# Attention and mixture-of-experts block on one core: the experts' fp32 products made of float32r parts, weights in three sets, and new places for all steps

## The chip, the core and the metric

The kernel runs on one core of one Trainium2 chip. The metric is the device time of one execution in microseconds. Five engines work from queues of their own, each in order: PE (TensorE) multiplies, DVE (VectorE), ACT (ScalarE) and POOL (GpSimd) do element-wise work, SP (SyncE) issues DMAs; POOL issues the indirect ones. Semaphores order them against each other.

## The reference, cut to what matters

```python
x = x + xattn(layernorm(x), ctx, ctx, w_q, w_kv, w_concat)      # x: 16 x 128 x 256, fp32
x = x + ffn(layernorm(x), ...)
# ffn: attn_out = layer_norm(x) * nw + nb
#      top-1 gate over 8 experts, capacity 2048 / 8 = 256 rows each
#      dispatched = the 256 rows (zeros where there are fewer) of each expert
h = gelu(einsum('ecm,emi->eci', dispatched, inter_w) + inter_b[:, None, :])    # 256 -> 1024
expert_out = einsum('eci,eim->ecm', h, output_w) + output_b[:, None, :]        # 1024 -> 256
moe_out = einsum('sec,ecm->sm', combine, expert_out)
rh = gelu(attn_out @ res_inter_w + res_inter_b)                 # the residual MLP, all rows
out = (rh @ res_output_w + res_output_b) * coef[:, :1] + moe_out * coef[:, 1:] + x
```

All operands are fp32.

## The kernel before

The 2048 rows are worked in 8 blocks of 256 (`U = 8`, two tiles `t` of 128 rows each). A block n < 8 goes through attention, gate and residual MLP. Its rows are then scattered into `dispatched` in DRAM by expert (POOL's indirect DMAs, step `gw`). When all blocks have been scattered, the 8 experts follow as n = 8 to 15, each with 256 rows. `weights(n)` gives the residual MLP's weights for n < 8 and a set of the expert's otherwise.

For one expert e (n = 8 + e):

- `ein`: SP loads the expert's rows (`drow`) and its bias (`outb`); PE transposes the rows (4 instructions, L607), ACT scales them into `ao` (L871, two instructions), DVE takes the row numbers (L1076).
- `up(n, c)`, c = 0 to 3: PE makes two 128-column pieces of the inner layer, each the sum of two fp32 products of 128x128 weights (stationary) with 128x256 values (`product`, L612); ACT applies the gelu to each (L890) and writes `h`.
- `down(n, t, q)`, t = 0, 1 and q = 0 to 3: PE adds two products of 128x128 pieces of `h` (stationary) with 128x256 of `w2` (L776). After q = 3, DVE adds the bias (L1093) and multiplies by the row's gate (L1097), and POOL adds the rows to the output by an indirect DMA (L580).
- `wload(e)`: SP loads w1 and w2 of the expert, 1 MB each; one semaphore stands for both. There are four sets (`SETS = 4`).

Which step comes after which is no result of the run: a table of times (`AT0`, `AT1`, `AT` for the blocks, `EXPERT` for the experts, `LOADS`, and a lag per engine) gives every step a planned time, and each engine issues its steps sorted by it. Only the order counts on the chip, not the planned times.

```python
    def order(lag):
        return [step for _, _, step in sorted((place + lag.get(step[0], [0.0])[0], n, step) for place, n, step in steps)]
```

In the middle of the expert stage PE's order is: up(n+1,0), down(n,0,0), down(n,0,1), up(n+1,1), down(n,0,2), down(n,0,3), up(n+1,2), down(n,1,0), ein, down(n,1,1), up(n+1,3), down(n,1,2), down(n,1,3).

The PSUM banks are rings of two per kind: `up` has one ring (`ubank`), freed by the gelu; `down` and the transposes share another (`mbank`).

## Time and profile before

| what | value |
|---|---|
| median of 3 runs | 447.14 us (445.47 to 448.82) |
| profiled execution, its own time | 447.72 us |
| its span | 446.0 us |
| PE busy | 381.6 us, 86% |
| ACT, POOL, DVE busy | 167.6, 153.2, 142.2 us |

The span runs from the first to the last instruction; 1.7 us of the execution's time lie outside it. An engine's busy time is the union of its instructions. PE's instructions overlap one another, so the mean duration of one is longer than the distance from one to the next.

### The profile page before, as it was taken

How to read it: one execution, taken by the hardware profiler on the slowest of the kernel's cores; microseconds unless marked ns; L12 is line 12 of the kernel's file. 1: busy time of each engine (PE TensorE's matmuls, PEld its weight loads, DVE VectorE, ACT ScalarE, POOL GpSimd, SP SyncE). 2: the span in 40 equal slices, each digit the busy share in tenths (PEclk: the TensorE clock that was granted, in tenths of full speed). 3: DMA queues.
4: the chain of work that ended last, by engine and by line, in shares of the span. 5: the costliest groups of instructions: out<-in, count | busy, mean ns of one | idle time of the engine just before them, and what ended most of it. 6: DMA issues, size and time to landing. Idle time of an engine off the chain costs nothing.

```text
span 446.0 us, 5656 instructions
## 1 busy us (share of the span) xinstructions
PE 381.6 (86%) x1978; PEld 292.7 (66%) x1978; DVE 142.2 (32%) x461; ACT 167.6 (38%) x325; POOL 153.2 (34%) x219
## 2 busy tenths in 40 slices
PE   4767777778998788988988988889999899999992
PEld 2435245555676476576576566678888788888881
DVE  3263424532354354363364263241101010101020
ACT  3213334345255435534536525552243223332310
POOL 4322313218156238247238035265002121212122
PEclk9757666986999999998999999999999999999998
DMA  7678650230022462381411410085122775581212
GB/s 203 189 193 233 228 134 2 76 79 24 23 72 77 125 234 71 94 272 51 114 35 61 104 37 12 21 294 165 47 68 64 196 235 166 128 251 12 25 18 29
DMA packets 51331, 49.78 MB, mean 112 GB/s; under 512 B 4764, under 2 KB 48488, under 8 KB 51304
## 3 DMA queue, kind: packets, MB, share of 16 engines
q1 hardware_dynamic: 48232, 45.21, 33.2%
q0 software_dynamic: 3072, 4.21, 5.2%
q8 instruction: 16, 0.26, 0.3%
q14 instruction: 11, 0.09, 0.1%
HBM read 33.65 MB, written 15.63 MB: 111 GB/s over the span
## 4 chain that ended last, share of the span: by engine, by line
PE 65%; DMA 10%; ACT 8%; DVE 7%; issue 5%; POOL 2%; SPq 2%; DVEq 0%; POOLq 0%; ACTq 0%
PE mbank L776 20%; PE ubank L612 18%; PE mbank L612 11%; DMA drow<-dispatched 8%; PE mbank L607 4%; PE pbank L697 4%; ACT p L847 3%; PE sbank L665 3%; PE sbank L687 3%; DVE smax L977 3%; PE pbank L706 2%; DVE core L1021 2%; ACT h L890 1%; DMA wq_raw<-in_L_xattn_w_q 1%; ACT oT L791 1%
## 5 line engine op out<-in xcount | busy, mean ns | idle before, releaser
L890 ACT ACTIVATE h<-ubank,vecT 128x256 f32<-128x256 f32 x128 | 53.7, 471 | 131.7 <-PE ubank L612 131.7
L776 PE MATMUL mbank<-w2r,h 128*128 128x256 f32 x256 | 64.1, 390 | 0.5 <-ACT h L890 0.5
L612 PE MATMUL ubank<-ao,w1r 128*128 128x256 f32 x256 | 62.7, 393 | 0.0
L776 PE MATMUL mbank<-w2e,h 128*128 128x256 f32 x256 | 60.8, 379 | 0.0
L580 POOL DMA_INDIRECT out_rows<-yrow,rowid x16 | 24.8, 1548 | 103.7 <-DVE yrow L1097 73.5
L612 PE MATMUL ubank<-ao,w1e 128*128 128x256 f32 x256 | 60.0, 379 | 0.0
L776 PEld LDWEIGHTS mbank<-w2r,h 128*128 128x128 f32 x256 | 48.4, 194 | 12.8 <-issue 5.3
L612 PEld LDWEIGHTS ubank<-ao,w1r 128*128 128x128 f32 x256 | 49.4, 197 | 6.6
L612 PEld LDWEIGHTS ubank<-ao,w1e 128*128 128x128 f32 x256 | 48.5, 190 | 6.6
L776 PEld LDWEIGHTS mbank<-w2e,h 128*128 128x128 f32 x256 | 48.2, 190 | 6.3
L977 DVE TENSOR_REDUCE smax<-sbank 128x4 f32<-128x512 f32 x64 | 41.9, 685 | 26.5 <-PE sbank L665 26.2
L847 ACT ACTIVATE p<-sbank 128x512 f32<-128x512 f32 x64 | 36.9, 595 | 33.8 <-PE sbank L687 33.7
L1093 DVE TENSOR_TENSOR ytmp<-mbank,outb 128x256 f32<-128x256 f32 x16 | 6.8, 425 | 90.8 <-PE mbank L776 90.8
L665 PE MATMUL sbank<-kstack,qstack 96*128 96x128 bf16 x256 | 25.0, 240 | 8.0 <-DVE smax L977 6.7
L665 PEld LDWEIGHTS sbank<-kstack,qstack 96*128 96x128 bf16 x256 | 18.9, 107 | 16.4 <-DVE smax L977 8.9
L687 PE MATMUL sbank<-qstack,kstack 98*128 98x512 bf16 x64 | 25.0, 418 | 2.2 <-DVE smax L977 1.8
L697 PE MATMUL pbank<-p,vone 128*32 128x512 f32 x128 | 19.1, 671 | 8.2 <-ACT p L847 7.8
L612 PE MATMUL mbank<-xT,wq 128*128 128x256 f32 x64 | 20.2, 470 | 4.2 <-ACT ao L871 3.0
L871 ACT ACTIVATE ao<-mbank,vecT 128x256 f32<-128x256 f32 x32 | 16.3, 561 | 15.3 <-PE mbank L607 15.3
L529 POOL TENSOR_TENSOR yy<-va,mhalf 128x4 f32<-128x4 f32 x8 | 8.4, 1046 | 39.7 <-DVE va L1012 39.7
L612 PE MATMUL mbank<-wc,oT 128*128 128x256 f32 x64 | 18.0, 429 | 4.2 <-ACT oT L791 4.2
L496 POOL TENSOR_TENSOR rs<-va,mhalf 128x2 f32<-128x2 f32 x8 | 5.8, 720 | 45.7 <-DVE va L936 45.7
(123 smaller groups left out, 438.1 us busy)
## 6 DMA issues: line engine op xcount, KB each, us to landing
w1e<-in_L_ffn_inter_w SPq DMA_DIRECT2D x8, 1024.0 KB, 4.9
w2e<-in_L_ffn_output_w SPq DMA_DIRECT2D x8, 1024.0 KB, 8.4
qstack<-dram_q SPq DMA_DIRECT2D x16, 384.0 KB, 4.6
dram_q<-qpart SPq DMA_DIRECT2D x8, 384.0 KB, 2.5
dispatched<-zrow SPq DMA_DIRECT2D x4, 516.0 KB, 5.4
drow<-dispatched SPq DMA_DIRECT2D x8, 258.0 KB, 8.3
xs<-in_x SPq DMA_DIRECT2D x8, 256.0 KB, 4.6
ctxs<-in_ctx SPq DMA_DIRECT2D x8, 256.0 KB, 4.7
```

The costliest lines, as they stand in the source:

```text
L580: pool.indirect_dma_start(out=out[:, :], in_=yrow[:, e % 2, t, :], in_offset=None, compute_op=ALU.add, out_offset=bass.IndirectOffsetOnAxi ...
L607: last = nc.tensor.transpose(dst[:, o:o + P], src[:, t, kc * P:(kc + 1) * P], ident[:, :])
L612: last = nc.tensor.matmul(dst, w[kc], v[kc], start=(kc == 0), stop=(kc == len(w) - 1))
L665: last = nc.tensor.matmul(b[:, i * P:(i + 1) * P], qstack[0:KS, r, t, 4 * (g % HG) + i, :], kstack[0:KS, r, bs], start=True, stop=True)
L687: nc.tensor.matmul(b[:, :], kstack[:, r, bs], qstack[:, r, t, hs:hs + 4, :], start=True, stop=True)\
L697: last = nc.tensor.matmul(b[32 * g:32 * g + 32, :, :], vone[:, u % 3, t, :], p32[:, n % 2, g, :, :], start=True, stop=True, tile_position= ...
L706: last = nc.tensor.transpose(b[:, i, :], o_raw[:, n % 2, i, :], ident[:, :])
L776: last = nc.tensor.matmul(b[:, 0:D], h[:, n % 2, f, t * P:(t + 1) * P], w2[:, f, :], start=(f == 0), stop=(f == FC - 1))
L847: nc.scalar.activation(p32[:, (k // HB) % 2, g % HB, :, :], scores, ACT.Exp, scale=SCALE)\
L871: ins = nc.scalar.activation(ao[:, n % NAO, kc, :], place["cT", n][:, kc * UT:(kc + 1) * UT], ACT.Identity, bias=vecT[:, R_NB + kc:R_NB + ...
L890: nc.scalar.activation(h[:, n % 2, f, :], place["up", n, c][:, j, :], ACT.Gelu_apprx_tanh, bias=vecT[:, col:col + 1]).then_inc(sem("gelu_d ...
L977: V.reduce_max(smax[:, g // HG, hs:hs + 4], place["A", u, g][:, :].rearrange("p (h t) -> p h t", h=4), AX)\
```

## The change

1. A product of an expert is no longer one fp32 product. Both operands are split into a high part (the value written as float32r) and a low part (the value less the high part), and three float32r products are added: high x high, high x low, low x high. The residual MLP and the attention stay as they were.
2. The splits: `ws1` (w1, in four quarters of 128x512: ACT copies the high part, POOL subtracts), `ws2` (w2, likewise: DVE copies, DVE subtracts), `ao` (ACT copies, DVE subtracts), and `h` after each `up` (ACT copies 128x512, DVE subtracts). The low part lies where the value lay; the high parts have tiles of their own, two of each.
3. Three sets of weights in place of four. w1 and w2 are loaded by steps of their own (`w1load`, `w2load`), each as soon as the last user of its own tile is through. `drow` and `outb` have four places in place of eight, so that `ein` of expert 4 and later waits for an earlier expert's end.
4. All planned times and lags are new, those of the attention too, and `o_rec` has two buffers.

```diff
-    SETS = 4
+    SETS = 3
+    EIN = 4
+    Q = 4
...
-        "period": 17.22, "up": [-2.35, 2.53, 4.67, 9.02],
-        "down": [17.16, 18.79, 20.45, 21.34, 23.58, 25.85, 26.32, 28.49], "ein": [9.47], "first": [-3.51],
+        "period": 13.91, "up": [-4.57, -1.85, -1.43, 2.78],
+        "down": [5.15, 7.92, 11.04, 14.37, 16.08, 16.88, 17.07, 17.83], "ein": [11.7], "first": [-2.28],
+        "ws1": [-23.13, -21.33, -21.16, -18.19], "ws2": [-6.23, -5.05, -3.84, 1.18], "w1load": [14.71],
+        "w2load": [36.23],
...
+            def w1load(e):
+                if e >= SETS:
+                    sp.wait_ge(sem("up_done"), C2 * (U + e - SETS + 1))
+                w1, src = (w1r, res_inter_w) if e < 0 else (w1e[e % SETS], inter_w[e])
+                sp.dma_start(w1[:, :, :], src.rearrange("(k p) f -> p k f", p=P))\
+                  .then_inc(sem("w1r_in" if e < 0 else f"w1e_in{e % SETS}"), 16)
+
+            def w2load(e):
+                if e >= SETS:
+                    sp.wait_ge(sem("down_done"), T * (U + e - SETS + 1))
+                w2, src = (w2r, res_output_w) if e < 0 else (w2e[e % SETS], output_w[e])
+                sp.dma_start(w2[:, :, :], src.rearrange("(c p) d -> p c d", p=P))\
+                  .then_inc(sem("w2r_in" if e < 0 else f"w2e_in{e % SETS}"), 16)
+
             def wload(e):
                 if e == 2:
                     sp.wait_ge(sem("x1_ready"), U)
-                if e >= SETS:
-                    sp.wait_ge(sem("down_done"), T * (U + e - SETS + 1))
-                w1, w2 = weights(U + e if e >= 0 else 0)
-                src1 = res_inter_w if e < 0 else inter_w[e]
-                src2 = res_output_w if e < 0 else output_w[e]
-                came = sem("wr_in" if e < 0 else f"we_in{e % SETS}")
-                sp.dma_start(w1[:, :, :], src1.rearrange("(k p) f -> p k f", p=P)).then_inc(came, 16)
-                sp.dma_start(w2[:, :, :], src2.rearrange("(c p) d -> p c d", p=P)).then_inc(came, 16)
+                w1load(e)
+                w2load(e)
...
+                if e >= EIN:
+                    sp.wait_ge(sem("y_ready"), T * (e - EIN + 1))
...
+            def split(e, q):
+                pool.wait_ge(sem("w1_high"), Q * e + q + 1)
+                w = quarter(w1e[e % SETS], q)
+                pool.tensor_tensor(quarter(w1l[e % SETS], q), w, quarter(w1h[e % 2], q).bitcast(f32), ALU.subtract).then_inc(sem("w1_low"), 1)
...
             def up(n, c):
                 w1 = weights(n)[0]
-                if c == 0:
-                    pe.wait_ge(sem("ao_ready"), n + 1)
-                    if n == 0:
-                        pe.wait_ge(sem("wr_in"), 32)
-                    if n >= U:
-                        e = n - U
-                        pe.wait_ge(sem(f"we_in{e % SETS}"), 32 * (e // SETS + 1))
-                b = claim("up", n, c)
-                for j in range(2):
-                    f = 2 * c + j
-                    last = product(b[:, j, :], chunks(w1, slice(f * P, (f + 1) * P)), chunks(ao[:, n % NAO, :, :]))
+                if n < U:
+                    if c == 0:
+                        pe.wait_ge(sem("ao_ready"), n + 1)
+                    if n == 0 and c == 0:
+                        pe.wait_ge(sem("w1r_in"), 16)
+                    b = claim("up", n, c)
+                    for j in range(2):
+                        f = 2 * c + j
+                        last = product(b[:, j, :], chunks(w1, slice(f * P, (f + 1) * P)), chunks(ao[:, n % NAO, :, :]))
+                else:
+                    e = n - U
+                    if c == 0:
+                        pe.wait_ge(sem("ao_low"), e + 1)
+                        pe.wait_ge(sem("w1_low"), Q * (e + 1))
+                    b = claim("up", n, c)
+                    for j in range(2):
+                        f = slice((2 * c + j) * P, (2 * c + j + 1) * P)
+                        wh, wl = chunks(w1h[e % 2], f), chunks(w1l[e % SETS], f)
+                        ah, al = chunks(aoh[:, e % 2, :, :]), chunks(aol[:, n % NAO, :, :])
+                        last = product(b[:, j, :], wh + wh + wl, ah + al + ah)
                 last.then_inc(sem("up_done"), 1)
 
             def down(n, t, q):
                 w2 = weights(n)[1]
+                e = n - U
                 if q == 0:
                     claim("down", n, t)
-                    pe.wait_ge(sem("gelu_done"), FC * (n + 1))
+                    if n < U:
+                        pe.wait_ge(sem("gelu_done"), FC * (n + 1))
+                        if n == 0:
+                            pe.wait_ge(sem("w2r_in"), 16)
+                    else:
+                        pe.wait_ge(sem("w2_low"), Q * (e + 1))
+                if n >= U and t == 0:
+                    pe.wait_ge(sem("h_low"), C2 * e + q + 1)
                 b = place["down", n, t]
                 for f in (2 * q, 2 * q + 1):
-                    last = nc.tensor.matmul(b[:, 0:D], h[:, n % 2, f, t * P:(t + 1) * P], w2[:, f, :],
-                                            start=(f == 0), stop=(f == FC - 1))
+                    if n < U:
+                        last = nc.tensor.matmul(b[:, 0:D], h[:, n % 2, f, t * P:(t + 1) * P], w2[:, f, :],
+                                                start=(f == 0), stop=(f == FC - 1))
+                    else:
+                        hi, lo = hh[:, e % 2, f, t * P:(t + 1) * P], hl[:, n % 2, f, t * P:(t + 1) * P]
+                        wh, wl = w2h[e % 2][:, f, :], w2l[e % SETS][:, f, :]
+                        nc.tensor.matmul(b[:, 0:D], hi, wh, start=(f == 0), stop=False)
+                        nc.tensor.matmul(b[:, 0:D], hi, wl, start=False, stop=False)
+                        last = nc.tensor.matmul(b[:, 0:D], lo, wh, start=False, stop=(f == FC - 1))
...
+                if n >= U:
+                    act.wait_ge(sem("ao_ready"), n + 1)
+                    if n >= U + 2:
+                        act.wait_ge(sem("up_done"), C2 * (n - 1))
+                    copy(aoh[:, n % 2, :, :], ao[:, n % NAO, :, :]).then_inc(sem("ao_high"), 1)
+
+            def split(e, q):
+                if q == 0:
+                    if e == 0:
+                        act.wait_ge(sem("x1_ready"), U)
+                    act.wait_ge(sem(f"w1e_in{e % SETS}"), 16 * (e // SETS + 1))
+                    if e >= 2:
+                        act.wait_ge(sem("up_done"), C2 * (U + e - 1))
+                copy(quarter(w1h[e % 2], q), quarter(w1e[e % SETS], q)).then_inc(sem("w1_high"), 1)
...
+                if n >= U:
+                    if n >= U + 2 and c == 0:
+                        act.wait_ge(sem("down_done"), T * (n - 1))
+                    act.wait_ge(sem("gelu_done"), 2 * (i + 1))
+                    copy(hh[:, n % 2, 2 * c:2 * c + 2, :], h[:, n % 2, 2 * c:2 * c + 2, :]).then_inc(sem("h_high"), 1)
...
+                dve.wait_ge(sem("ao_high"), e + 1)
+                a = ao[:, (U + e) % NAO, :, :]
+                V.tensor_tensor(aol[:, (U + e) % NAO, :, :], a, aoh[:, e % 2, :, :].bitcast(f32), ALU.subtract).then_inc(sem("ao_low"), 1)
+
+            def split(e, q):
+                if q == 0:
+                    if e == 0:
+                        dve.wait_ge(sem("x1_ready"), U)
+                    dve.wait_ge(sem(f"w2e_in{e % SETS}"), 16 * (e // SETS + 1))
+                    if e >= 2:
+                        dve.wait_ge(sem("down_done"), T * (U + e - 1))
+                w = quarter(w2e[e % SETS], q)
+                V.tensor_copy(quarter(w2h[e % 2], q), w).then_inc(sem("w2_high"), 1)
+                dve.wait_ge(sem("w2_high"), Q * e + q + 1)
+                V.tensor_tensor(quarter(w2l[e % SETS], q), w, quarter(w2h[e % 2], q).bitcast(f32), ALU.subtract).then_inc(sem("w2_low"), 1)
+
+            def up(n, c):
+                if n < U:
+                    return
+                i = C2 * (n - U) + c
+                dve.wait_ge(sem("h_high"), i + 1)
+                a = h[:, n % 2, 2 * c:2 * c + 2, :]
+                V.tensor_tensor(hl[:, n % 2, 2 * c:2 * c + 2, :], a, hh[:, n % 2, 2 * c:2 * c + 2, :].bitcast(f32), ALU.subtract)\
+                    .then_inc(sem("h_low"), 1)
```

Sorted by the new tables, one expert of the middle reads, engine by engine (n = 11 is expert 3):

```
PE    up(11,0) down(10,0,2) up(11,1) up(11,2) ein(4) down(10,0,3) up(11,3) down(10,1,0..3) down(11,0,0..1) up(12,0)
ACT   up(11,0) ws1(4,3) up(11,1) up(11,2) ein(4) up(11,3) ws1(5,0..2) up(12,0)
DVE   up(11,0) ws2(3,3) down(10,0) up(11,1) up(11,2) ein(4) down(10,1) up(11,3) ws2(4,0..2) up(12,0)
POOL  ws1(4,0..2) down(10,0) ws1(4,3) down(10,1) ws1(5,0..2)
SP    w1load(5) w2load(4) ein(5) w1load(6) w2load(5) ein(6)
```

Ahead of the experts PE's order is now up(7), ein(0), down(7,0), down(7,1,0), up(8,0), down(7,1,1) and so on; before it was up(7), ein(0), all of down(7), up(8,0). On ACT ws1(0) stands between the steps of up(7), ahead of ein(0); on DVE ws2(0) begins behind down(7,0). In the attention, SP now issues the residual MLP's weights (`wload` of -1) directly ahead of gather(2,0), the load of block 2's queries, where it stood ahead of the first maxima of block 1 before, and PE runs the transpose M of a middle block behind q of a later one, where it stood ahead of it.

## Rows read from the trace of the kernel before

**Rows 1.** The page: span, and busy time of each engine.

```profile
span 446.0 us, 5656 instructions
PE 381.6 (86%) x1978; PEld 292.7 (66%) x1978; DVE 142.2 (32%) x461; ACT 167.6 (38%) x325; POOL 153.2 (34%) x219
```

**Rows 2.** Busy time by stretch: its length, PE, PEld, DVE, ACT, POOL; clock; DMA.

```profile
0.00:286.00 286.00, 235.00 (x1281) 165.79 (x1282) 120.07 (x385) 121.59 (x223) 112.03 (x176) 0.89 0.36 107
...
320.80:437.40 116.60, 114.50 (x541) 99.47 (x539) 13.27 (x38) 33.91 (x78) 23.23 (x15) 1.00 0.43 113
```

**Rows 3.** The chain that ended last, in order of time: start, us, what.

```profile
310.45 2.58 DMA drow<-dispatched
313.81 7.14 PE mbank L776 x32
```

**Rows 4.** The same chain from 400 us on.

```profile
402.40 1.73 PE ubank L612 x8
404.13 1.73 PE mbank L776 x8
...
411.90 0.44 PE mbank L607 x4
...
428.74 8.65 PE mbank L776 x40
```

**Rows 5.** Timeline of PE in the attention: start, length of the group, count.

```profile
255.57 0.61 PE L665 MATMUL sbank<-kstack,qstack 96*128 96x128 bf16 x8
256.02 0.61 PE L706 MATMUL pbank<-ident,o_raw 128*128 128x128 f32 x4
```

**Rows 6.** Single durations by tile (ns, min/median/max), answers for kstack, w1e and ident.

```profile
L665 PEld LDWEIGHTS sbank<-kstack,qstack x256: 95/98/152, 24.6 to 266.7; 96*128 96x128 bf16 x128
...
L612 PEld LDWEIGHTS ubank<-ao,w1e x256: 186/190/192, 320.6 to 428.1; 128*128 128x128 f32 x128
...
L607 PEld LDWEIGHTS mbank<-ident,drow x32: 138/141/144, 313.1 to 412.0; 128*128 128x128 f32 x32
```

**Rows 7.** Timeline of ACT in the expert stage.

```profile
336.97 0.84 ACT L890 ACTIVATE h<-ubank,vecT 128x256 f32<-128x256 f32 x2 [2.61 <-PE ubank L612]
338.27 1.02 ACT L871 ACTIVATE ao<-mbank,vecT 128x256 f32<-128x256 f32 x2 [0.46 <-PE mbank L607]
```

**Rows 8.** Groups by line, engine and shape: count, busy us, mean ns, idle before.

```profile
L580 POOL DMA_INDIRECT out_rows<-yrow,rowid x16 | 24.8, 1548 | 103.7 <-DVE yrow L1097 73.5 <-DVE rowid L1076 30.1
...
L1093 DVE TENSOR_TENSOR ytmp<-mbank,outb 128x256 f32<-128x256 f32 x16 | 6.8, 425 | 90.8 <-PE mbank L776 90.8
...
L1097 DVE TENSOR_SCALAR yrow<-ytmp,drow 128x256 f32<-128x256 f32 x16 | 5.7, 353 | 0.6
...
L954 DVE TENSOR_TENSOR qres<-mbank,qpart 128x512 f32<-128x512 f32 x8 | 5.5, 692 | 27.8 <-ACT qpart L791 27.8
...
L791 ACT ACTIVATE qpart<-qres 128x512 bf16<-128x512 f32 x8 | 5.0, 628 | 3.0 <-DVE qres L954 3.0
```

**Rows 9.** Timeline: DVE's gate steps beside POOL, at two places.

```profile
243.59 1.15 POOL L523 TENSOR_TENSOR qpart<-qres,qpart 128x512 bf16<-128x512 f32 x1
...
243.82 0.96 DVE L1039 SCALAR_TENSOR_TENSOR gkey<-gd,desc 128x16 f32<-128x16 f32 x1
...
298.11 2.56 POOL L538 TENSOR_SCALAR xs<-xs,oneplus,mrs 128x256 f32<-128x256 f32 x2
...
298.91 0.18 DVE L1039 SCALAR_TENSOR_TENSOR gkey<-gd,desc 128x16 f32<-128x16 f32 x1
```

**Rows 10.** Single durations by tile (min/median/max), answer for xs: DVE's tensor_scalar.

```profile
L1021 DVE TENSOR_SCALAR core<-xs,mv,yy x16: 384/540/884, 70.4 to 294.5; 128x256 f32<-128x256 f32 x16
```

**Rows 11.** DMA issues by line: count, KB each, median us from issue to landing.

```profile
w1e<-in_L_ffn_inter_w SPq DMA_DIRECT2D x4, 1024.0 KB, 4.9
w2e<-in_L_ffn_output_w SPq DMA_DIRECT2D x4, 1024.0 KB, 8.4
```

**Rows 12.** Busy time by stretch, as in rows 2, near the kernel's start.

```profile
20.00:40.00 20.00, 14.45 (x70) 9.69 (x70) 9.39 (x20) 4.29 (x9) 4.61 (x7) 0.50 0.67 181
```

More of the change, by code:

```diff
@@ L115, in xattn_moe_ffn_kernel @@
-        "ein": [0.0], "down": [0.25], "zero": [0.0], "late": [-0.64],
+        "load": [3.74], "kspill": [-7.59], "qspill": [-1.22], "gather": [11.52], "M": [0.79], "wload": [-0.23],
+        "ein": [-7.33], "down": [4.67], "zero": [2.93], "late": [-3.31], "w1load": [0.0], "end": [0.19],
+        "small": [0.72], "w2load": [-3.58],
     }
     LOADS = {
-        "late": [-70.79], "vec": [-39.4], "zero": [-46.04, -45.13, -6.03, -0.66],
-        "weights": [0.5, 14.17, 15.87, 27.03, 27.11],
+        "late": [-84.53], "vec": [17.26], "zero": [-38.12, -21.43, -12.78, -4.6],
@@ L588, in _ @@
             calls = {"small": small, "ln1": ln1, "xn": norm_x, "kv": k_parts, "qlast": q_last, "ln2": ln2, "core": residual,
[L589 removed]
+                     "gw": scatter, "bias": bias, "ws1": split, "down": down, "end": end}
             for step in order(LAG_POOL):
```

128 lines of the change are left out of this document (74 added, 54 removed), and 21 rows, old and new, of tables (AT, AT0, AT1).

## The prediction

> **What bounds the kernel now.** I read the page first: PE is busy for 86% of the span, no other engine for 40% [rows 1]. The stretches show where: in the expert stage (320.8 to 437.4 us, 116.6 us) PE is busy for 98% at full clock (granted 1.00, the 2.4 GHz level), ACT for 34 us, POOL 23, DVE 13 [rows 2]. The chain in order of time says the same: from 400 us on it is PE alone, groups of 8 matmuls 1.73 us apart [rows 4]. So one instruction of an expert's product costs 1.73 / 8 = 0.216 us. An expert has 64 of them (each of its 32 products is recorded as two) and four transposes in 0.44 us [rows 4]: 64 x 0.216 + 0.44 = 14.3 us, against 116.6 / 8 = 14.6 measured. The stage costs what PE's passes cost. Ahead of it stands a latency chain through the last block's scatter and the load of the first expert's rows, which land at 313.0 us [rows 3]; the change does not touch it; the attention (286 us, PE busy for 235 [rows 2]) is touched only in its order.
>
> **PE's new price.** A product becomes three float32r matmuls. No trace here shows one. The nearest rows: a bf16 matmul of 128 columns, each with new weights, takes 0.45 / 8 = 0.056 us [rows 5], one pass at 0.44 ns a column; an fp32 instruction of 256 columns takes 0.216, or 0.84 ns a column, two passes. So float32r is between one pass, 0.108 us, and two, 0.216. I take one pass: a format that still needed two would be no format of its own, and three of them would be half again as dear as the fp32 product. Its weight load may show. The load of 128 fp32 columns takes 190 ns as a record and lies wholly behind 0.216 us of streaming; the transposes' single load takes 141 ns at a distance of 0.44 / 4 = 0.11 us; a bf16 load takes 98 at a distance of 0.056 [rows 4 to 6]. In all three the distance is that of the streaming alone, so I take the load as hidden. If it were not, the 128 columns of the load would add their 0.056 to each. Per expert: 96 x 0.108 + 0.44 = 10.8 us, 3.5 less than now.
>
> **ACT's new load**, in order with all it did: gelu 4 x 0.84, affine 1.02 [rows 7], and nine copies of 128x512 (four of w1, four of h, one of ao) at the 0.628 us of the copy of qres [rows 8]: 3.4 + 1.0 + 5.7 = 10.1 us, perhaps 0.2 more for the waits on its own results. That is just under PE. Its copies of h stand between the gelu and the next gelu, which frees PE's bank: a step `up` takes ACT 0.84 + 0.65 = 1.5 us and PE 12 x 0.108 = 1.3, but the down steps lie between, so it holds.
>
> **DVE's new load.** Nine subtractions of 128x512 at 0.69 us (L954) [rows 8]; four copies of 128x512, between 0.48 (the 0.353 of a 128x256 tensor_scalar [rows 8] plus half of the 0.26 that a tensor_tensor takes for 256 more columns, 0.692 - 0.425) and 0.69, as a subtraction; I take 0.55. Two bias additions and two multiplications, 2 x (0.425 + 0.353) [rows 8], and the row numbers, 0.2. Sum 6.2 + 2.2 + 1.6 + 0.2 = 10.2, with a wait of 0.03 ahead of some ten of them 10.5 us (10.2 to 11.1). What stands behind a waiting instruction matters here: DVE waits for PE's down(10,0) and only then does the subtractions of up(11,1) and up(11,2) and of ein(4).
>
> **POOL's new load.** Four subtractions at 1.15 (L523) [rows 9] and two indirect DMAs at 1.55 [rows 8]: 7.7 us. POOL's last quarter of w1 stands behind the scatter of down(10,0), so up(12,0) needs, after PE's last matmul of down(10,0): 0.8 on DVE, 1.55 and 1.15 on POOL, 3.5 us and up to two of DVE's instructions in between. PE has up(11,3), down(10,1) and two steps of down(11,0) for that, 48 matmuls, 5.2 us. It fits while nothing else delays it.
>
> **The two together.** This is what decides. DVE's gate step L1039 handles 16 numbers a row and takes 0.18 us in one place and 0.96 in another. In the slow place POOL runs a tensor_tensor from 243.59 to 244.74, and L1039 ends at 244.78; in the fast one POOL runs a tensor_scalar [rows 9]. Both L1039 and POOL's tensor_tensor read two operands from SBUF. DVE's tensor_scalar shows it too: 384 ns at least, 884 at most [rows 10], where the slow ones stand beside POOL's arithmetic. So DVE's two-operand work does not run beside POOL's two-operand work. The change puts 9 x 0.69 = 6.2 us of the first on DVE and 4 x 1.15 = 4.6 of the second on POOL for each expert, and the four copies and two multiplications (2.9 us) may be held up like the tensor_scalar. If all of it excludes, DVE and POOL together need 10.5 + 4.6 = 15.1 us, less what DVE can do meanwhile (the additions from PSUM, 0.85, and the row numbers), 14.1. If only the two-operand work excludes, the copies and multiplications also fit beside POOL: 11.2, but then they must fall in the right place. I take 13.3 us per expert, nearer the upper end because the long copies resemble the tensor_scalar that was held up.
>
> The Trainium skill (SBUF — State Buffer, Who interferes with whom) says that a DVE instruction with two SBUF inputs contends with a GpSimd instruction that reads SBUF, that a copy in a 2-port mode takes the same ports, and that the later one blocks fully. The first holds here beside the tensor_tensor, not beside the tensor_scalar, where L1039 kept its 0.18 us [rows 9]. By the rule everything excludes, the period would be 14.1 and the time 441.7.
>
> **Loads.** An expert's w1 lands 4.9 us after its issue and w2 8.4 [rows 11]. w1 is now issued when its set's up steps end, a full period before ACT splits it, and w2 about as early: 4.9 and 8.4 of 13. Hidden, also by the three sets; uncovered it would cost what the period falls short of, nothing here. `ein` of expert 4 on waits for an end three experts back, long past; behind it on SP stand only loads that are as late themselves.
>
> **Start and end of the stage.** The first expert's rows land at 313.0 and, ein(0) done, down(7) begins at 313.8 [rows 3]. up(8,0) now stands behind 5/8 of down(7), 20 matmuls at 0.216, so it starts at 313.8 + 4.3 = 318.1. The splits it needs can be made while the last block's chain runs, when ACT, POOL and DVE have room. From there seven periods, then the last expert: its up and down, 96 x 0.108, the six steps of the expert before that still follow, 36 x 0.108, and 0.3 of waits, 14.6 us. End of PE: 318.1 + 7 x 13.3 + 14.6 = 425.8, before 437.4 [rows 4]: 11.6 us less.
>
> **The attention.** The work is the same; the order differs. Block 2's queries now queue behind the residual MLP's 2 MB, by the experts' loads (8.4 us for the pair [rows 11]) up to some 6 us later once, with eight score steps of block 1 to cover it. M behind q rather than ahead of it comes later by q's eight instructions, 8 x 0.216 = 1.7 us a block, where nothing else covers the maxima's round trip. The buffers of `o_rec` may give back a few tenths. I take 0, between -4 and +5.
>
> Sum: 447.7 (the profiled execution, 0.6 above the median) - 11.6 = 436.1, predicted 436.
>
> **Rivals.**
> - *DVE and POOL don't get in each other's way* (the large operands interleave, or the steps fall apart in time). Then PE's 10.8, ACT's 10.3 and DVE's 10.5 stand almost level, and with three engines in step the period is some 11.6: 318.1 + 81.2 + 14.6 = 413.9, time 424. For it: L1039 is a tiny operation, and nothing here shows a long subtraction beside POOL. Against: the slow L1039 row, which ends 0.04 us after POOL's instruction [rows 9].
> - *The gain is eaten whole.* Full exclusion, 14.1, and the in-order queues (DVE waiting for PE's down while POOL is free, then both at once) add half a microsecond or more: 14.6 to 15, time 445 to 448. It is also what the Trainium skill's rule, named above, leads to.
> - *The clock falls, and it gets slower.* PE's busy share drops from 98% to 10.8 of 13.3, 81%, in short pieces. Between 20 and 40 us PE is busy for 72% at a granted clock of 0.50, the 1.2 GHz level [rows 12]. At that level an expert costs PE 21.4 us. The point from which it decides: with a share s of the stage's time at 1.2 GHz the period is 1 / ((1 - s) / 13.3 + s / 21.4); it reaches 14.6 at s = 0.23, and with s = 0.5 it is 16.4, the last expert 18: 450.9, time 461. Against it: the attention's middle is busy to a like degree, in pieces, at a clock of 0.89 over 286 us that includes the slow start [rows 2].
> - *Float32r is no single pass or its weight load shows.* At 0.108 + 0.056 an expert takes 16.2 us, time about 464; at two passes 21.2, time above 500. The change then does not do what it says.
>
> **Chances.** Forecast with its neighbourhood (periods 12.5 to 14.3, 430 to 443) 0.45; no interference (420 to 430) 0.25; eaten whole (443 to 450) 0.16; clock 0.06; float32r dearer 0.06; attention order worse by more than it is here allowed 0.02. The range for 8 in 10 goes from 422 to 449: it leaves out the two slow cases and the low tip of the fast one. A difference of 1%, 4.5 us, is about what a measurement of this kernel can tell (its three runs lie 3.4 apart). Below 442.7: 0.25 and most of 0.45, together 0.67; within 1%: 0.19; above: 0.14.
>
> **What would show it.** The matmuls of L612 and L776 in the expert stage 0.108 us apart, loads hidden. The expert period near 13.3 with PE idle ahead of up or down for 2 to 3 us an expert, ended by DVE's low parts of h or POOL's of w1. DVE's subtractions at 0.69 where alone and up to 1.15 longer beside POOL's. up(8,0) at 318. Clock at 1.00. The last residual addition of the attention (block 7) where it is now, within 5 us. Wrong would be: DVE's subtractions all at 0.69 (first rival), ACT the last to be waited for (its copies dearer than 0.63), PE's distance other than 0.108, or an attention that has moved by more than the experts.

## The result, and the profile after

The changed kernel takes 415.87 us (median of 4 runs, 414.37 to 416.36) against 447.98 (445.47 to 449.9) in the same comparison: ratio 0.928, 95% interval 0.923 to 0.934, 32 us faster. I had predicted 436, between 422 and 449. The profiled execution took 416.18 us.

The page of the kernel after: span, busy time of each engine, the chain by line.

```profile
span 414.4 us, 6411 instructions
PE 353.6 (85%) x2234; PEld 286.6 (69%) x2234; DVE 228.7 (55%) x565; ACT 203.7 (49%) x395; POOL 196.4 (47%) x251
...
PE ubank L656 13%; PE mbank L838 11%; PE mbank L656 10%; DVE w2h L1179 8%; PE sbank L709 4%; PE mbank L651 3%; DVE w2l L1181 3%; PE mbank L843 3%; PE pbank L741 3%; PE mbank L845 3%; PE mbank L844 3%; PE sbank L731 2%; DMA qstack<-dram_q 2%; DMA kstack<-dram_k 2%; DVE hl L1189 2%
```

Against [rows 1] PE is busy 28 us less and DVE, ACT and POOL more, DVE by 86.5 us. Read like that, the gain seems to be the cheaper products. The milestones say something else. They are starts in the two timelines: the residual addition of a block (`xs<-xs,mbank`, L1003 before, L1093 after), the first transpose of the first expert's rows, the first product of an expert, the end of PE.

| milestone, us | before | after | after less before |
|---|---|---|---|
| residual addition, block 0 | 64.3 | 59.0 | -5.3 |
| block 2 | 130.3 | 108.8 | -21.5 |
| block 3 | 161.3 | 137.0 | -24.3 |
| block 4 | 194.3 | 174.6 | -19.7 |
| block 7 | 290.8 | 257.2 | -33.6 |
| first expert's rows transposed | 313.2 | 282.5 | -30.7 |
| up(8,0) | 320.8 | 288.7 | -32.1 |
| end of PE | 437.4 | 405.5 | -31.9 |

The row of block 7 in the timeline of DVE after:

```profile
257.19 0.69 DVE L1093 TENSOR_TENSOR xs<-xs,mbank 128x512 f32<-128x512 f32 x1 [4.19 <-PE mbank L656]
```

So the whole gain is made before the experts begin, in the part whose work did not change. The expert stage took 116.6 us [rows 2] and takes 116.8; of the 11.6 us that I forecast, 8.9 belonged to it and 2.7 to its start:

```profile
288.70:405.50 116.80, 103.35 (x810) 101.40 (x808) 97.70 (x142) 69.47 (x142) 58.71 (x41) 0.96 0.49 132
```

(Length, busy time of PE, PEld, DVE, ACT and POOL, granted clock, DMA share and GB/s, as in rows 2.)

**Why the stage did not get shorter.** The chain of the kernel after, in order of time, within one expert of the middle:

```profile
314.80 0.69 DVE w2l L1181
315.49 4.80 DVE w2h L1179
320.31 0.69 DVE w2l L1181
321.38 0.69 DVE w2l L1181
322.07 0.60 DVE hl L1189
323.08 0.57 issue
323.65 0.43 DVE ytmp L1207
324.12 0.39 PE mbank L843
```

Where [rows 4] had PE alone, the chain is now mostly DVE, and from 315 us on each of five experts in a row has one copy of w2 (L1179) of 4.8 us in it. The same line takes 0.42 us when it is let through, and the timeline shows what runs beside a long one (single durations by tile, ns, min/median/max; then the timeline of the kernel after):

```profile
L1179 DVE CAST w2h<-w2e x32: 411/420/4906, 288.7 to 393.7; 128x512 fp32r<-128x512 f32 x32
```

```profile
345.59 4.89 DVE L1179 CAST w2h<-w2e 128x512 fp32r<-128x512 f32 x1
...
345.85 4.34 POOL L612 TENSOR_TENSOR w1l<-w1e,w1h 128x512 fp32r<-128x512 f32 x3
```

The copy ends 0.3 us after the third of three subtractions that POOL runs without a gap (4.34 us, their starts some 1.25 apart), not after the first. All five long copies look like this one: by the records each starts some 0.25 us ahead of the first subtraction, while POOL's scatter is under way. Behind it on DVE stand the low part of h, the next quarters of w2 and the bias addition that frees PE's bank. It is not so beside every run of three. At the start of the stage DVE's instructions and POOL's took turns:

```profile
299.94 4.44 POOL L612 TENSOR_TENSOR w1l<-w1e,w1h 128x512 fp32r<-128x512 f32 x3 [6.01 <-ACT w1h L859]
299.98 1.53 DVE L1179 CAST w2h<-w2e 128x512 fp32r<-128x512 f32 x1
...
301.55 1.67 DVE L1181 TENSOR_TENSOR w2l<-w2e,w2h 128x512 fp32r<-128x512 f32 x1
...
303.15 1.51 DVE L1179 CAST w2h<-w2e 128x512 fp32r<-128x512 f32 x1
```

There POOL's records hardly overlap one another (0.04 us); beside the long copies they overlap by 0.6. What decides between the two, no run shows. What the bias addition waits for in the stage, and what PE waits for (us in total, times, longest):

```profile
DVE ytmp L1207 <- PE mbank L845: 16.0, 10, 2.5
...
PE mbank L843 <- DVE ytmp L1207: 13.4, 6, 2.6
```

The clock follows some of these halts. After the one that ends at 338.91 the matmuls of the timeline are 0.12 us apart for a while and then 0.21, from 340.60 to 343.81:

```profile
340.20 0.28 PE L844 MATMUL mbank<-w2l,hh 128*128 128x256 f32 x1
340.32 0.28 PE L845 MATMUL mbank<-w2h,hl 128*128 128x256 f32 x1
...
341.67 0.41 PE L843 MATMUL mbank<-w2h,hh 128*128 128x256 f32 x1
341.89 0.41 PE L844 MATMUL mbank<-w2l,hh 128*128 128x256 f32 x1
```

Of the six windows of 15 us from 305 to 395 us, three with such a piece have a granted clock of 0.89, the others 1.00. The pieces follow the first, third and sixth of the six halts (1.8, 2.6 and 2.6 us); the second, fourth and fifth (2.1, 1.8 and 2.6 us) brought none. Those 15 matmuls cost 15 x 0.094 = 1.4 us. So an expert of the middle costs 96 x 0.119 + 0.44 = 11.9 us of matmuls, 2.2 of halts (13.4 / 6) and 0.7 of clock (3 x 1.4 / 6): 14.8. The transposes of `drow` of the last six experts lie 14.0 to 16.2 us apart, 14.9 in the mean.

**Where the attention's time came from.** What PE waited for over five middle blocks, before (130 to 291 us), then after (100 to 257 us):

```profile
PE mbank L607 <- DVE core L1021: 4.4, 5, 1.7
PE pbank L697 <- ACT p L847: 4.4, 6, 1.0
PE mbank L612 <- ACT ao L871: 3.4, 4, 1.0
PE mbank L612 <- ACT oT L791: 3.4, 5, 1.1
PE sbank L665 <- DVE smax L977: 2.3, 4, 0.6
...
PE pbank L706 <- ACT o_raw L791: 0.7, 2, 0.5
```

```profile
PE sbank L709 <- issue: 5.6, 1, 5.6
PE mbank L656 <- ACT oT L859: 1.1, 2, 0.8
PE mbank L717 <- DVE smax L1065: 0.8, 1, 0.8
```

The answer for before sums to 19.1 us with two more rows of 0.3 and 0.2, the one for after to 8.1 with two of 0.4 and 0.2. Five blocks took 290.8 - 130.3 = 160.5 us and take 148.4: 12.1 less, of which 11.0 are these waits. Nearly every middle block had the same handful of halts of 0.4 to 1.7 us, each on a short round trip through ACT or DVE; in the new order other matmuls stand in most of these places. Up to block 2, where 21.5 us went, PE's waits fell from 23.8 us (20 to 130 us) to 17.4 (20 to 100 us), 9.9 of them on gathers, and the clock comes on top. The busy time by stretch, before, then after:

```profile
60.00:80.00 20.00, 15.12 (x76) 10.17 (x76) 7.81 (x18) 6.99 (x13) 5.51 (x9) 0.73 0.19 44
80.00:100.00 20.00, 14.08 (x75) 10.89 (x74) 8.21 (x35) 8.37 (x15) 3.81 (x8) 0.87 0.31 85
```

```profile
60.00:80.00 20.00, 17.02 (x104) 11.62 (x101) 10.90 (x29) 8.22 (x16) 3.13 (x5) 0.83 0.46 125
80.00:100.00 20.00, 18.35 (x108) 14.10 (x107) 10.35 (x53) 10.42 (x23) 14.61 (x22) 1.00 0.33 86
```

From 40 to 120 us the granted clock averaged 0.77 before and 0.91 after, worth up to 12 us of full speed in 80. What is left after is the row of 5.6 us: the timeline has PE idle ahead of 163.55, and one more piece of 2.9 us ahead of 64.7. Both wait for the gather of a block's queries; for the first the profile names no releaser, but the gather issued at 159.39 landed at 163.46. SP's timeline after shows what was ahead of it:

```profile
146.05 0.52 SPq L451 DMA_DIRECT2D dram_q<-qpart  x1
...
148.21 0.42 SPq L418 DMA_DIRECT2D w1e<-in_L_ffn_inter_w  x1
148.68 1.31 SPq L425 DMA_DIRECT2D w2e<-in_L_ffn_output_w  x1
150.09 1.74 SPq L451 DMA_DIRECT2D dram_q<-qpart  x2
...
159.39 0.58 SPq L463 DMA_DIRECT2D qstack<-dram_q  x1
```

Two megabytes of weights, the first of which is split only from 278.7 us on, stand between two spills of the queries. The spills behind them took 8 us to land, where the median of all is 2.7, and SP waited 6.8 us at the gather for them. At 54.25 and 54.97 the residual MLP's weights stand in the same way directly ahead of the gather of block 2.

### The profile page after: what moved, and what is told of

Its sections match the earlier page's. It is cut to its first block, busy times and chain, and to the rows that moved or that the text cites. A ratio compares the mean times of both kernels' runs of the same rounds, so it can differ in the third digit from the quotient of the medians.

```text
span 414.4 us, 6411 instructions
## 1 busy us (share of the span) xinstructions
PE 353.6 (85%) x2234; PEld 286.6 (69%) x2234; DVE 228.7 (55%) x565; ACT 203.7 (49%) x395; POOL 196.4 (47%) x251
## 4 chain that ended last, share of the span: by engine, by line
PE 56%; DVE 17%; DMA 9%; issue 5%; SPq 5%; ACT 3%; POOL 2%; POOLq 0%; DVEq 0%
PE ubank L656 13%; PE mbank L838 11%; PE mbank L656 10%; DVE w2h L1179 8%; PE sbank L709 4%; PE mbank L651 3%; DVE w2l L1181 3%; PE mbank L843 3%; PE pbank L741 3%; PE mbank L845 3%; PE mbank L844 3%; PE sbank L731 2%; DMA qstack<-dram_q 2%; DMA kstack<-dram_k 2%; DVE hl L1189 2%
## 5 line engine op out<-in xcount | busy, mean ns | idle before, releaser
L612 POOL TENSOR_TENSOR w1l<-w1e,w1h 128x512 fp32r<-128x512 f32 x32 | 47.2, 1669 | 12.2 <-ACT w1h L859 12.2
L843 PE MATMUL mbank<-w2h,hh 128*128 128x256 f32 x128 | 39.2, 306 | 13.4 <-DVE ytmp L1207 13.4
L709 PEld LDWEIGHTS sbank<-kstack,qstack 96*128 96x128 bf16 x256 | 19.4, 109 | 30.7 <-issue 25.7
L1179 DVE CAST w2h<-w2e 128x512 fp32r<-128x512 f32 x32 | 38.9, 1215 | 0.0
L844 PE MATMUL mbank<-w2l,hh 128*128 128x256 f32 x128 | 38.2, 298 | 0.0
L845 PE MATMUL mbank<-w2h,hl 128*128 128x256 f32 x128 | 38.1, 297 | 0.0
L843 PEld LDWEIGHTS mbank<-w2h,hh 128*128 128x128 f32 x128 | 26.4, 206 | 14.7 <-DVE ytmp L1207 14.7
L845 PEld LDWEIGHTS mbank<-w2h,hl 128*128 128x128 f32 x128 | 26.5, 207 | 0.0
L844 PEld LDWEIGHTS mbank<-w2l,hh 128*128 128x128 f32 x128 | 26.4, 206 | 0.0
L656 PE MATMUL ubank<-aoh,w1h 128*128 128x256 f32 x128 | 26.4, 287 | 0.0
L656 PE MATMUL ubank<-aoh,w1l 128*128 128x256 f32 x128 | 25.6, 282 | 0.0
```

Source lines behind the costliest of these rows:

```text
L612: pool.tensor_tensor(quarter(w1l[e % SETS], q), w, quarter(w1h[e % 2], q).bitcast(f32), ALU.subtract).then_inc(sem("w1_low"), 1)
L656: last = nc.tensor.matmul(dst, w[kc], v[kc], start=(kc == 0), stop=(kc == len(w) - 1))
L709: last = nc.tensor.matmul(b[:, i * P:(i + 1) * P], qstack[0:KS, r, t, 4 * (g % HG) + i, :], kstack[0:KS, r, bs], start=True, stop=True)
L843: nc.tensor.matmul(b[:, 0:D], hi, wh, start=(f == 0), stop=False)
L844: nc.tensor.matmul(b[:, 0:D], hi, wl, start=False, stop=False)
L845: last = nc.tensor.matmul(b[:, 0:D], lo, wh, start=False, stop=(f == FC - 1))
```

## The experiments

Three questions: which half of the change gives the gain; what in the attention's order does; what holds the expert stage at its old length. Letters in the expectations name theories, the main ones being: A, that the new order of the attention is the gain and the splits give nothing; C, that DVE and POOL in each other's way set the expert period; F, that the place of `gw` and `bias` sets the wait for `core`; G, that single moves in the old order don't add up. "Residual addition 7" is the milestone of the table above.

**Order alone.** The kernel after, with the experts' products in plain fp32 again, without any split.

```diff
-                if n < U:
+                if c == 0 and n >= U:
+                    pe.wait_ge(sem(f"w1e_in{(n - U) % SETS}"), 16 * ((n - U) // SETS + 1))
+                if True:
...
-                     "ein": rowids, "ws2": split, "up": up, "down": down}
+                     "ein": rowids, "down": down}
```

> The changed kernel with its new order of all steps, its loads by halves and its three sets, but the experts' products as plain fp32 (no splits, no float32r). Theory A (the whole gain is the attention's new order; the expert stage costs the same either way, since DVE and POOL exclude each other): 415 to 419 us, expert stage 116 to 118 us. Rival (the float32r products carry a good part of the gain): 425 or more.

413.23 us (412.07 to 417.82), a little below the expected range, ratio 0.929 (0.921 to 0.937). Residual addition 7 at 258.2, expert stage 117.6 us. Half of the change, the half that my forecast valued at 0, gives all of the gain.

**Splits with the old order.** The tables, lags and loads of before; the experts' own table and the splits of after. The lags that the experts' `up` and `down` share with the blocks' are the old ones.

```diff
-    PERIOD = 31.57
-    OWN = [0.0, 14.0, 43.08, 72.66]
+    PERIOD = 32.0
+    OWN = [0.0, 15.16, 39.23, 67.63]
...
-        "small": [-0.62], "vec": [-0.1], "up": [0.5], "ws2": [-2.7], "xn": [0.06], "qlast": [-6.17],
...
+        "ein": [-0.72], "up": [0.5], "ws2": [-2.7],
```

> The changed kernel with the planned times and lags of the attention, and the times of the loads, as they were before; the float32r products, the splits and the experts' new order stay. Theory A: 443 to 450 us, the last block's residual sum at 290 us as before. Rival: 435 or less.

462.82 us (462.02 to 464.02), ratio 1.041 (1.032 to 1.050): a miss, 13 us above the expected range. The attention ended as before (residual addition 7 at 288.8); the stage took 135.1 us, at a granted clock of 0.90. Its waits from 340 to 440 us:

```profile
DVE hl L1194 <- ACT hh L864: 25.9, 7, 4.8
...
PE mbank L848 <- DVE ytmp L1212: 22.5, 5, 4.6
```

With the experts' table but without its lags DVE stands before the subtraction of h until ACT has copied it, and PE behind DVE. So this kernel had changed two things. The next has the experts' lags too.

**Splits with the old order, experts' lags new.**

```diff
+        def at(place, step):
+            late = step[0] in ("ein", "ws1", "ws2", "w1load", "w2load") or step[0] in ("up", "down") and step[1] >= U
+            return place + (new if late else lag).get(step[0], [0.0])[0]
```

> As e2_split_only, but the experts' steps keep the changed kernel's lags, so that only the attention goes by the times and lags of before. Theory A: the attention ends as before (block 7's residual sum at 288 to 291 us) and the stage takes 115 to 119 us as in the changed kernel: 443 to 449 us. Rival (the junction with the old attention costs the experts something of its own): 452 or more.

442.61 us (10 runs, 441.26 to 445.53), ratio 0.998 (0.994 to 1.001). Residual addition 7 at 286.3, a little ahead of what was expected, stage 116.4. The float32r experts alone change nothing that can be measured; the same splits in a poorer order cost 20 us. This kernel also has the three sets, the separate loads and the second `o_rec` of after, so none of these gives the gain by itself. The clock of the attention goes with the order too: from 40 to 120 us it is 0.81 here and 0.91 with the new order alone.

**One buffer for `o_rec`.**

```diff
-                if n >= 2:
-                    dve.wait_ge(sem("o_ready"), n - 1)
+                if n >= 1:
+                    dve.wait_ge(sem("o_ready"), n)
```

> The changed kernel with one buffer of o_rec, as before. Theory A (only the order matters): within 1 us of 415.9. Rival (the second buffer frees DVE in the softmax's tail): 3 us or more above it.

415.16 us (413.06 to 416.66), ratio 0.933 (0.925 to 0.942), as the kernel after. The second buffer does nothing.

**Weights out of the gathers' way.** Only two planned times, so that SP issues them behind the gathers of the queries.

```diff
-        "weights": [26.33, 27.47, 37.5, 41.94, 61.05],
+        "weights": [27.1, 41.9, 37.5, 41.94, 61.05],
```

> The changed kernel with two loads of weights issued later: the residual MLP's behind gather(2,1) rather than ahead of gather(2,0), expert 0's behind gather(5,1) rather than between block 5's query spills. Theory B (2 MB ahead in the queues delay the next block's queries; PE stands 3.1 us at 64.7 and 5.8 us at 163.6 for it): 408 to 411 us. Rival (another wait takes its place): 414 to 416.

400.1 us (398.08 to 402.17), ratio 0.901 (0.893 to 0.909): 15.8 us below the kernel after and 15.1 below `o_rec_one`, which ran in the same comparison; more than expected. Residual addition 2 at 101.1, 7 at 240.8, stage 117.1. SP's timeline now has each load behind the gathers; at block 5, from the second gather on:

```profile
145.33 0.58 SPq L463 DMA_DIRECT2D qstack<-dram_q  x1
145.95 0.78 SPq L418 DMA_DIRECT2D w1e<-in_L_ffn_inter_w  x1
```

SP's longest wait at a gather is 1.5 us, and PE's wait of 5.6 is gone. Between the two profiles the attention is 16.4 us shorter. 2.2 of these are there at block 0, before the moved load can act: kernels with this order of the attention reach that point between 56.7 and 59.8 us. Another 5.5 are there by block 2, and 8.6 come at block 4. The two halts were 2.9 and 5.6, so some 5.6 of the 14.1 are what they drew after them. The clock can account for that: in the kernel after it was granted at 0.50, the 1.2 GHz level, from 64.0 to 70.8 and from 163.0 to 169.8 us, which costs up to 3.4 us each time; here it stays at 1.00 from 42 us to the end of the attention.

**One known halt taken out of the old order.** In before, POOL did `gw` and `bias` of block 0 ahead of `core` of block 1; here they stand behind it. In the middle blocks `bias` stood between `ln2` and `core` of the next block; here it goes ahead of both, and on ACT and DVE `gw` goes ahead of the second `o`.

```diff
-        "bias": [23.76], "up": [17.62, 19.37, 22.16, 25.97],
+        "bias": [5.5], "up": [17.62, 19.37, 22.16, 25.97],
```

> The kernel before with two steps of its attention moved: gw of block 0 behind core of block 1 (DVE and ACT no longer hold block 1's normalised rows behind the gate's exponent, where PE stood 3.5 us), and gw and bias of every middle block earlier, so that POOL's arithmetic no longer lies beside DVE's core. Theory F (the attention's gain is made of such bare waits, each removable by itself): 3.5 us once and 0.5 to 0.9 us for each of six blocks, 436 to 441 us on a base of 444 to 447. Rival G (the pitch of a block is set by PE's whole work, and a removed wait reappears as another): within 2 us of the kernel before.

Ratio 0.989 (0.981 to 0.996), 5 us, with 2 to 8 inside the interval; median 439.78 against 445.93. The halt on `core` in the middle blocks falls from 4.4 us in five times to 2.1 in two.

**Two more halts taken out.** The same kernel, with q and PV later on PE.

```diff
-        "core": [0.0], "gate": [0.0], "loc": [0.06], "A": [0.0], "B": [0.0], "PV": [0.0], "part": [0.0], "up": [0.0],
-        "down": [0.0], "oT": [0.0], "proj": [0.0], "M": [0.61], "q": [0.0], "kv": [0.0], "vt": [0.0], "xT": [0.0],
+        "core": [0.0], "gate": [0.0], "loc": [0.06], "A": [0.0], "B": [0.0], "PV": [1.45], "part": [0.0], "up": [0.0],
+        "down": [0.0], "oT": [0.0], "proj": [0.0], "M": [0.61], "q": [0.7], "kv": [0.0], "vt": [0.0], "xT": [0.0],
```

> b_gw_bias with two more steps of PE put elsewhere: q of a later block behind up(n,3) in place of ahead of it, and the second PV of a block behind the last down step in place of ahead of it. In b_gw_bias PE stands 1.16 us bare ahead of q and 0.85 ahead of that PV in every middle block. Theory F (each bare wait can be removed by itself): 6 x (1.16 + 0.6) = 10 us less than b_gw_bias, 428 to 433. Rival G (the wait reappears elsewhere, since what waits is a chain from block to block and not PE's order): 436 to 441.

441.71 us (440.1 to 446.14), ratio 0.992 (0.989 to 0.996): no further gain. PE's waits from 125 to 285 us:

```profile
PE mbank L612 <- DVE qres L954: 3.5, 3, 1.2
PE pbank L706 <- ACT o_raw L791: 2.3, 6, 0.8
...
PE pbank L697 <- ACT p L847: 1.6, 2, 1.0
PE mbank L612 <- ACT ao L871: 0.4, 1, 0.4
```

The wait for `ao` went from 3.4 to 0.4 us and that for `p` from 4.4 to 1.6, as meant. In their place stand `qres` with 3.5, which was not there, and `o_raw` with 2.3 in place of 0.7. The list sums to 16.2 us, and to 16.7 without the two moves. These two moves exchanged one round trip for another; the order of after has found places for all of them together. A second cause can't be excluded: the granted clock was 0.94 to 0.97 in three of the four windows of 40 us from 125 us on, where without the two moves it was 1.00 throughout.

**w2's high part copied on ACT.** DVE is relieved of the copy that POOL holds up.

```diff
+                copy(quarter(w2h[e % 2], q), quarter(w2e[e % SETS], q)).then_inc(sem("w2_high"), 1)
...
-                V.tensor_copy(quarter(w2h[e % 2], q), w).then_inc(sem("w2_high"), 1)
```

> The changed kernel with the copy of w2's high part on ACT in place of DVE, nothing else. Theory C (in each expert DVE's copy waits 4.5 us until POOL's run of three subtractions is over, and that sets the expert period): the period falls from 14.8 to 12.5 to 13.3 us, the stage from 116.8 to 101 to 107, time 400 to 407. Rival D (DVE's subtractions with two SBUF operands wait for POOL just as the copy does): each wait only changes its place; 3 us of DVE's work are gone, 1.7 of them while POOL is idle: time 411 to 416.

402.16 us (401.22 to 404.1), ratio 0.901 (0.896 to 0.905). Stage 106.0, period 13.1, clock 1.00 in all five windows of 15 us from 300 us on. But now one subtraction of w2 in five experts waits for the rest of POOL's run (durations by tile):

```profile
L1189 DVE TENSOR_TENSOR w2l<-w2e,w2h x32: 675/692/3258, 287.3 to 384.8; 128x512 fp32r<-128x512 f32 x32
```

**w1's low part subtracted on DVE.** DVE gets 4 x 0.69 us more work per expert, at new places in its queue (a lag of 2.0 for `ws1`); POOL does nothing but its indirect DMAs.

```diff
-                     "gw": scatter, "bias": bias, "ws1": split, "down": down, "end": end}
+                     "gw": scatter, "bias": bias, "down": down, "end": end}
...
+            def low1(e, q):
+                dve.wait_ge(sem("w1_high"), Q * e + q + 1)
+                w = quarter(w1e[e % SETS], q)
+                V.tensor_tensor(quarter(w1l[e % SETS], q), w, quarter(w1h[e % 2], q).bitcast(f32), ALU.subtract).then_inc(sem("w1_low"), 1)
```

> The changed kernel with the subtraction of w1 on DVE in place of POOL: DVE's own work rises by 2.8 us an expert, and nothing on POOL but the output's scatters is left to exclude it. Theory C: DVE's 9.8 + 2.8 us plus its waits for PE make a period of 13 to 14 us, time 402 to 411. Rival D gives the same; rival E (the period is set by the in-order waits between PE and DVE, not by DVE's time): no gain or worse, 416 to 425.

396.22 us (394.77 to 398.58), ratio 0.889 (0.883 to 0.895), better than expected. Stage 100.6, period 12.3. Nothing on DVE is held up any more; a copy beside a scatter of POOL takes 0.50 us in place of 0.42 (durations by tile, then a window of the stage):

```profile
L1174 DVE CAST w2h<-w2e x32: 417/421/501, 284.5 to 373.4; 128x512 fp32r<-128x512 f32 x32
L1176 DVE TENSOR_TENSOR w2l<-w2e,w2h x32: 691/693/695, 285.0 to 373.9; 128x512 fp32r<-128x512 f32 x32
```

```profile
345.00:360.00 15.00, 14.77 (x125) 14.56 (x125) 13.80 (x28) 10.50 (x22) 4.95 (x3) 1.00 0.66 164
```

DVE does more and is waited for less: PE's halts on `ytmp` between 300 and 385 us sum to 2.0 us, and PE is busy for 98% at full clock. With 11.9 us of matmuls an expert, little is left to win here. The median is 19.7 us below the kernel after, which was measured in another comparison; by the two ratios it is 17. The stage is 16.2 shorter. The attention, whose order was not touched, ended 3.9 us earlier in this profile. Part of that is the spread between executions: with the same order and loads it ended at 256.1, 256.2, 257.2 and 258.2 us in the profiles of `o_rec_one`, `w2_act`, the kernel after and `e1_order_only`. The rest has no cause that these runs show.

**Both together.** `w1_dve` with the two planned times of `loads_moved`.

> w1_dve and loads_moved in one kernel. Theory (the two gains lie in different stages and add): 415.9 - 15.8 - 19.7 = 380.4 us, within 2 us. Rival (with the attention 15 us shorter, weights or the first splits come too late for the expert stage): 386 or more.

383.6 us (381.51 to 385.18) against 444.58, ratio 0.866 (0.859 to 0.873). Residual addition 7 at 241.1, stage 100.5. The two gains add up but for 3 us, outside the 2 us expected and short of the rival's 386; 3 us is about what `w1_dve` had from an attention that happened to end early. This version beats both kernels.

**What sets a float32r matmul's distance.** The version above, the last expert's `up` as matmuls of 128 columns: twice as many, half as wide.

```diff
-                        last = product(b[:, j, :], wh + wh + wl, ah + al + ah)
+                        for x in (slice(0, UT),) if n < N - 1 else (slice(0, P), slice(P, UT)):
+                            last = product(b[:, j, x], wh + wh + wl, [v[:, x] for v in ah + al + ah])
```

> best, with each float32r matmul of the last expert's four up steps run as two of 128 columns in place of one of 256 (96 matmuls in place of 48). What sets the 0.119 us between float32r matmuls? If the weight load does: again 0.119 us apart, the last expert's up steps 5.7 us longer. If the streaming at one pass a column does: 0.056 to 0.065 us apart, no longer. If a narrow float32r matmul falls back to more passes: 0.11 us (two) or 0.21 us (four) apart.

389.56 us in one execution. The chain from 350 us on:

```profile
362.05 5.31 PE ubank L651 x48
```

48 matmuls of 128 columns in 5.31 us are 0.111 us apart, against 0.119 with 256 columns. Half the columns save 0.008 us, so streaming at one pass does not set the distance at 128 columns; a load of weights that cannot be shorter than 0.11 us, or a narrow form that needs two passes, would both give this. The trace of the kernel before speaks for the load. It has matmuls of only 10 columns, each with 128x128 new fp32 weights:

```profile
242.17 1.06 PE L612 MATMUL mbank<-wg_raw,ao 128*128 128x10 f32 x8
```

They start 0.112 us apart with next to nothing to stream, and the record of their weight load is 192 ns long, as is that of the 128-column float32r matmuls here. Two passes are not excluded by that. What makes the wide form's 0.119 out of a load of 0.11 and a streaming of 0.108 stays open.

## Why the prediction was wrong

**The step that failed** is the one on the attention: "The work is the same; the order differs. ... I take 0, between -4 and +5." It measured -33.6 us (residual addition 7), and `e1_order_only` shows that this order alone gives the whole gain. I had costed two moves that I could see (a later M, a gather behind weights) and taken the rest of the new order as neutral, with no reason given. The experts, for which I forecast 11.6 us, gave nothing measurable in `split_alone`, so two misses of opposite sign partly hid each other: with the experts' gain the time would have been farther below the forecast. I read PE's share in the attention, 235 of 286 us [rows 2], as leaving little to win, and that was wrong in two ways. The 51 us in which PE was not busy were four times the gain that I worked out for the experts, and I asked of none of them what ended it; PE's waits from 130 to 291 us alone are 19.1 us, in rows that I could have asked for. And PE's busy time is a union of records that are longer than the distance between them (after: 0.28 us against 0.12), so the start of each halt is covered by the end of the record before it: a middle block went from 33.0 to 27.8 us at full clock in both, and PE's busy time in it from 29.40 to 27.43 with the same work. The Trainium skill (Perfetto Trace Analysis, Identifying the Most-Contended Engine) says that the matmul busy share is not a good measure of how close PE is to its limit, and names in its place the FLOPs done against the peak and the share of the weight loads. The second holds here: PEld's share was 165.79 / 286 = 58% in the attention and 99.47 / 116.6 = 85% in the expert stage [rows 2]; in a middle block it went from 21.94 of 33.0 us before to 20.91 of 27.8 after.

**The clock in the attention.** I used the granted clock of 0.50 between 20 and 40 us [rows 12] only as evidence on the expert stage. It was also time to be won: up to 12 us between 40 and 120 us (0.77 before, 0.91 after). In that window itself little changed, 0.58 after.

**PE's price** was mis-sized: 0.119 us, not 0.108; 11.9 us of matmuls an expert, not 10.8. That a wide float32r matmul needs no two passes (0.216) came true. The rows did not show that the load is hidden, as I had it. I read the transposes' distance of 0.11 us as streaming alone, but the fp32 matmuls of 10 columns shown above (L612) are as far apart, so a load of 128x128 fp32 weights already takes about 0.11, more than the 0.108 that I priced. The load of float32r has a like record, 188 ns. In the clock rival, twice 10.8 is 21.6 and not 21.4; nothing hangs on it.

**ACT** was right: its copies took 0.61 to 0.64 us, and it was hardly ever the last to be waited for.

**DVE.** Subtractions 0.69, as taken; the copy 0.42, below the lower bound of 0.48; so DVE alone needs 9.7 us without its waits, where I had 10.2. **POOL.** Its subtractions start 1.25 us apart and not 1.15, and a scatter takes 1.69 in the mean and not 1.55: 8.4 us an expert, not 7.7.

**The two together.** The mechanism was right and its size was not: 13.3 us an expert expected, 14.9 measured. I counted how much of the two engines' work excludes the other, as if they took turns instruction by instruction. They do so at the start of the stage, but in five experts one copy waits for POOL's whole run, and what stands behind it in DVE's queue waits with it, the bias addition that frees PE's bank among them: 2.2 us a time on PE. The Trainium skill (SBUF — State Buffer, Who interferes with whom) has the exclusion of a copy in a 2-port mode and of an instruction with two inputs from SBUF, and both are shown here: 4.89 us for a copy of 0.42, 3.26 for a subtraction of 0.69. It says that whoever issues first keeps the ports for the whole instruction; here they stayed with POOL for three instructions in a row, although by the records the copy had started first. That this copy runs in a 2-port mode, no view names. With POOL's arithmetic gone the period is 12.3, which shows that this, and not PE's price or the loads, held it at 14.9.

**The rival "the gain is eaten whole"** (period 14.6 to 15) is what happened in the stage. Some 0.7 us of the period is what the clock rival named: pieces of 3.2 us at the 1.2 GHz level, in three windows of six. The clock fell after three of six halts of 1.8 to 2.6 us; in the two kernels whose halts are 1.0 us at most (`w2_act`, `w1_dve`) it stays at 1.00.

**Start of the stage.** From the start of down(7) to up(8,0) I took 4.3 us for 20 matmuls. The chain has 5.53:

```profile
282.46 1.09 PE mbank L651 x4
283.55 5.53 PE mbank L838 x20
```

The four transposes ahead of them took 1.09 us where [rows 4] has 0.44: PE had halted for the first expert's rows and came back at the lower clock.

**Loads.** "Hidden", I wrote of the experts' weights, and "nothing here"; that is true of the experts that use them. What they cost is what stands behind them in SP's queue, some 15 us, as large as what POOL's subtractions cost the stage. Of the residual MLP's load I had expected "up to some 6 us later once, with eight score steps of block 1 to cover it"; the gather took 7.95 us and PE stood for 2.9, and then ran at half the clock for 6.8. The experts' first load, 94 us further on, I did not look at.

**M behind q**, costed at up to 1.7 us a block, shows as one wait of 0.8 us in five blocks (L717 above). **`o_rec`**: nothing, as taken.

**Open.** Which of the moves in the attention carry the gain. One pair was shown to be worth 5 us alone (2 to 8), two more moves nothing on top of it. A kernel with the new tables for the first blocks and the old for the rest, or the reverse, was not tried.

## What to carry to other kernels

When a change re-sorts all steps, cost the sorting first: list what the bounding engine waits for over a few periods, sum it, and take that sum, with the clock that halts cost, as what a new order can win; on TensorE do it from waits and the share of weight loads, not from the busy share. A large load with no one waiting for it is not free if a small dependent transfer stands behind it in the queue: put it behind the gathers. Where work on VectorE and on GpSimd exclude each other, try it on one of the two, even the busier one: here 2.8 us more work on VectorE made each expert 2.5 us shorter.

## What the runs showed of the hardware

- A VectorE copy of 0.42 us beside three back-to-back subtractions of GpSimd from SBUF ended after the last of them in five experts: up to 4.91 us. A subtraction with two operands from SBUF did too (3.26 us). At the start of the stage the two engines took turns instead (1.53, 1.67, 1.51 us). GpSimd's indirect DMAs did not hold VectorE like that: with these alone no copy took over 0.50 us and no subtraction of w2 over 0.695.
- A float32r matmul of 256 columns with new weights each time follows the last after 0.119 us, one of 128 columns after 0.111; an fp32 matmul of 10 columns with new 128x128 weights after 0.112. An fp32 product of 256 columns took two instructions of 0.216 us [rows 4], three float32r ones 0.357: 17% less time of PE, for 13 copies and 13 subtractions of 128x512 an expert.
- Of six halts of PE of 1.8 to 2.6 us in a stage otherwise full, three were followed, 1.0 to 1.7 us after their end, by 3.2 us at half the clock. With halts of 1.0 us at most the clock stayed at 1.00.
